# A gated decoder of sixteen blocks on one core: first three layers and last layer reordered, weight splits behind the second mixing, first attention tile's exponential in two halves

## The chip, the cores and the metric

One NeuronCore of one Trainium2 chip runs the whole program in one launch. The metric is the device time in microseconds. The kernel before took 381.14, 376.11 and 380.48 us in three runs, median 380.48.

## The reference

Two sequences of 512 tokens with 128 channels (`x`) go through four layers. Each layer is a cross attention to 77 context tokens and a feed-forward block, each behind a layer norm and a gate. In outline:

```
layer 0: bidirectional attention flow (similarity, softmax, product with tokens) | RWKV channel mix
         xk = mu_k*h + (1-mu_k)*h_prev ; r = sigmoid(xr Wr') ; out = r * (relu(xk Wk')^2 Wv')
layer 1: two-way attention with interpolation and gate                           | mixture of 8 experts, gelu, top 2
layer 2: 16-head attention with the mask                                         | mixture of 8 experts, silu, grouped top 2
layer 3: 16-head attention without a mask                                        | 8 small units relu(w1*u+b1)*w2, summed, projected
x = x + tanh(g) * block(layernorm(x))   after every block
```

All is float32 in and out.

## The kernel before, in words

The two sequences are the two halves (b = 0, 1) of every step. `x[b]` holds a half as 4 tiles of 128 tokens. A block of a half is: statistics on VectorE (DVE), the power -0.5 on GpSimd (POOL, `norm`), the normalised `h` on VectorE (`normalised`), transposes on TensorE (PE), a copy to `hT` on ScalarE (ACT, `transposed`), and then the products. Norm k and `transposed(k)` belong to block k // 2 of half k % 2.

Every engine has its program written out by hand, and each engine runs it strictly in that order. Semaphores join them. There is no scheduler; an operation whose data is ready stands behind every earlier one of its engine.

TensorE's order mixes the halves and holds filler matmuls (`keep_busy(bank, n)`, `heat` in the rows, L1443), whose result nobody reads, in places where it would otherwise wait.

The expert stages. Expert weights are loaded by SyncE (SP) into `up_raw`, `down_raw`. ScalarE rounds them (`up_hi`, `down_hi`), GpSimd makes the rests (`split_up` L460, `split_down` L467), and each product is three matmuls (L1436 to L1438). In step g VectorE makes the rest of an activation (`rlo`, L1229). At steps 15, 16, 19 and 21 it also multiplies an expert's output by that expert's routing weights (`weigh_copied`, L1173 and L1175), and TensorE's down projection of step g waits for `rlo` of step g. The routing weights reach VectorE as rows on all partitions: SyncE stores them to DRAM (`rowd`, L337), waits until the store has landed, and loads each row to 128 partitions (`rowB`, L351).

SyncE's queue, in its order:

```
load experts 0, 1; wait q["dl"] and load experts 2, 3; wait kv["one"]
50 DMAs: pieces of the values vN of layers 2 and 3 into vals (L376), up to 77 rows x 2 x 8 each
store rowd for half 0, four rowB loads; store rowd for half 1, four rowB loads; then rows and experts in turn
```

`kv["one"]` is raised by GpSimd behind four operations that write ones into `vals` (L495). `m["split"]` is raised by VectorE in `parts`, which splits `hT` into `hhi` and `hlo` (L1127, L1128) ahead of an expert stage; its first call is `parts(6, 0)`.

In layer 0's feed-forward block `mixed(b)` makes the two mixed inputs by L1012 (difference), L1013 (key) and L1015 (receptance). `l1["x"]` counts the mixed inputs, two per half.

In the attentions of layers 2 and 3 (`attend(n)`) eight tiles u of 128 tokens follow each other: scores (L1816), maximum and subtraction in two pairs of banks on VectorE (L1286, L1289), exponential on ScalarE (L812), ten transposes (L1829), copies (L826), product with the values (L1847).

The last block has eight units. `unit` (L887) makes them on ScalarE; `own_unit` (L1393, L1395) makes two of each half on VectorE. Four go one by one through TensorE (`direct`, L1967), four are summed on VectorE first (`summed`, L1403, L1406) and then projected (`from_sums`, L1985).

Of the kernel before, what the change touches and what calls it, by code (L numbers as in the profile page):

```python
# [82 lines left out]
def flamingo_program(nc, a, out):  # L83

    ctx = ExitStack()
    with ctx:
# [159 lines left out]
        l3 = {n: sem(f"l3_{n}") for n in ["wout", "s", "ss", "u", "ua", "ud", "up", "acc", "out"]}  # L246
# [171 lines left out]
        def _(pool):  # L418
# [155 lines left out]
        def _(act):  # L574
# [30 lines left out]
            def down_hi(i, p, chunks, nd, sems):  # L605

                if i > 0:
# [105 lines left out]
            second_T(1)  # L713
            transposed(6)
            first_exp(1)
# [74 lines left out]
            def attend(n):  # L790
# [18 lines left out]
                for u in range(NT * B):  # L809
                    T = NT * B * n + u  # L810
                    act.wait_ge(at["sub"], NG * (T + 1))
                    nc.scalar.activation(Sx[T % 2][:, 0:SPAN], Sx[T % 2][:, 0:SPAN], ACT.Exp).then_inc(at["exp"], 1)  # L812
# [76 lines left out]

            act.wait_ge(l3["ss"], 1)  # L890
# [10 lines left out]
        def _(dve):  # L901
# [64 lines left out]
            def softmax_out(b, exp_sem, P_sem, sumcol):  # L966
# [4 lines left out]
                link(V.reciprocal(small[b][:, sumcol + NT:sumcol + 2 * NT], small[b][:, sumcol:sumcol + NT]))  # L971
                V.tensor_tensor(pr, pr, small[b][:, sumcol + NT:sumcol + 2 * NT].unsqueeze(2).broadcast_to([P, NT, K]),
                                ALU.mult).then_inc(P_sem, 1)

# [34 lines left out]
            def mixed(b):  # L1009
# [4 lines left out]
                                       ALU.add).then_inc(l1["x"], 1)  # L1014
                V.scalar_tensor_tensor(W4_[b][:, :], W1_[b][:, :], col("mu_r"), hTz[b][:, 0:S], ALU.mult,  # L1015
# [53 lines left out]
            mixed(0)  # L1069
            from_outputs(1)  # L1070
            squared(0)
# [5 lines left out]
            mixed(1)  # L1077
# [310 lines left out]
            def own_unit(b, j):  # L1388

                dve.wait_ge(l3["ss"], b + 1)  # L1390
                dve.wait_ge(at["T"], 3 * (2 * NT * B - 1 + b))
                i, u = DIRECT[2 * j], Sx[b][:, j * S:(j + 1) * S]
                link(V.tensor_scalar(u, W1_[b][:, :], cols[:, C_W1 + i:C_W1 + i + 1], cols[:, C_B1 + i:C_B1 + i + 1],  # L1393
# [37 lines left out]
        def _(pe):  # L1431
# [69 lines left out]
            def output(b, tiles):  # L1501

                pe.wait_ge(l0["W"], b + 1)
                pe.wait_ge(l0["u"], b + 1)
                for t in tiles:
                    o = tile(bank[4 * b + 1], t)
                    mm(o, tile(hT[b], t), w14[b][:, :], start=True, stop=False)
                    mm(o, W2_[b][0:K, t * P:(t + 1) * P], ctxW2[:, b, :], start=False, stop=False)
# [582 lines left out]
```

## Time and profile before

| | |
|---|---|
| median of the runs | 380.48 us (376.11 to 381.14) |
| the profiled execution | 380.25 us |
| its span | 378.5 us |
| TensorE, VectorE, ScalarE, GpSimd busy | 354.4, 280.2, 213.2, 103.9 us |
| mean granted clock of TensorE | 0.985 |

The span starts at the first recorded instruction, and all times in rows count from there. TensorE's clock is given as a share of 2.4 GHz; 0.50 is 1.2 GHz. A float32 matmul is recorded in passes, so TensorE's counts are twice those of the program there. Busy times of TensorE are modelled from its records, and some records can be missing.

### The profile page before, as it was taken

How to read it: one execution, taken by the hardware profiler on the slowest of the kernel's cores; microseconds unless marked ns; L12 is line 12 of the kernel's file. 1: busy time of each engine (PE TensorE's matmuls, PEld its weight loads, DVE VectorE, ACT ScalarE, POOL GpSimd, SP SyncE). 2: the span in 40 equal slices, each digit the busy share in tenths (PEclk: the TensorE clock that was granted, in tenths of full speed). 3: DMA queues.
4: the chain of work that ended last, by engine and by line, in shares of the span. 5: the costliest groups of instructions: out<-in, count | busy, mean ns of one | idle time of the engine just before them, and what ended most of it. 6: DMA issues, size and time to landing. Idle time of an engine off the chain costs nothing. (4 is left out here: it accounts for less than half of the span.)

```text
span 378.5 us, 5695 instructions
## 1 busy us (share of the span) xinstructions
PE 354.4 (94%) x2020; PEld 266.4 (70%) x2034; DVE 280.2 (74%) x644; ACT 213.2 (56%) x389; POOL 103.9 (27%) x106
## 2 busy tenths in 40 slices
PE   6999989989999999989899999999989989999996
PEld 2667586857777888854688886667667646789765
DVE  5477978589776777786777769687767867788485
ACT  1315344567978889752466654767455514566382
POOL 6211751011344546220112101214556323000220
PEclk9999998999999999999999999999999998799999
DMA  6800120000474323000001100065350000000001
GB/s 192 291 3 0 51 66 5 4 5 4 132 217 158 90 76 82 5 0 2 0 2 43 42 2 0 0 189 163 97 167 2 0 2 0 0 3 2 0 2 55
DMA packets 18676, 20.37 MB, mean 54 GB/s; under 512 B 7119, under 2 KB 10729, under 8 KB 18649
## 3 DMA queue, kind: packets, MB, share of 16 engines
q1 hardware_dynamic: 18100, 19.52, 17.1%
q0 software_dynamic: 96, 0.32, 0.3%
q8 instruction: 16, 0.26, 0.3%
q10 hardware_dynamic: 453, 0.18, 0.2%
q14 instruction: 11, 0.09, 0.1%
HBM read 19.26 MB, written 0.59 MB: 52 GB/s over the span
## 5 line engine op out<-in xcount | busy, mean ns | idle before, releaser
L1229 DVE TENSOR_TENSOR rlo<-banks,rhi 128x512 fp32r<-128x512 f32 x64 | 44.0, 691 | 20.0 <-ACT rhi L744 19.1
L442 POOL TENSOR_TENSOR rstd<-var,neghalf 128x4 f32<-128x4 f32 x16 | 16.6, 1040 | 132.2 <-DVE var L918 132.2
L1436 PE MATMUL banks<-hhi,wuh 128*128 128x512 f32 x128 | 51.4, 402 | 0.6 <-DVE hlo L1128 0.5
L750 ACT ACTIVATE banks<-banks,b1s 128x512 f32<-128x512 f32 x64 | 42.4, 662 | 15.8 <-PE banks L1438 15.5
L1438 PE MATMUL banks<-hhi,wul 128*128 128x512 f32 x128 | 50.0, 391 | 0.0
L1437 PE MATMUL banks<-hlo,wuh 128*128 128x512 f32 x128 | 49.9, 390 | 0.0
L1436 PE MATMUL banks<-rhi,wdh 128*128 128x512 f32 x96 | 40.6, 423 | 8.2 <-DVE rlo L1229 3.4
L1443 PE MATMUL banks<-heat 128*128 128x512 bf16 x124 | 36.2, 408 | 4.1 <-POOL heat L420 2.9
L1847 PEld LDWEIGHTS banks<-vals,shared 128*128 128x128 f32 x320 | 37.7, 193 | 0.7 <-ACT shared L826 0.6
L826 ACT ACTIVATE shared<-banks 128x512 f32<-128x512 f32 (+1 forms) x48 | 23.7, 526 | 25.6 <-PE banks L1829 25.4
L1847 PE MATMUL banks<-vals,shared 128*128 128x27 f32 (+1 forms) x320 | 37.8, 271 | 0.1
L1437 PE MATMUL banks<-rlo,wdh 128*128 128x512 f32 x96 | 37.6, 391 | 0.0
L1438 PE MATMUL banks<-rhi,wdl 128*128 128x512 f32 x96 | 37.6, 391 | 0.0
L460 POOL TENSOR_TENSOR wul<-up_raw,wuh 128x512 fp32r<-128x512 f32 x16 | 21.6, 1348 | 51.9 <-ACT wuh L603 50.7
L846 ACT ACTIVATE shared<-banks 128x512 f32<-128x512 f32 x32 | 19.2, 599 | 29.4 <-PE banks L1438 29.1
L1286 DVE TENSOR_REDUCE small<-banks 128x8 f32<-128x616 f32 x32 | 25.4, 794 | 13.7 <-PE banks L1816 13.7
L1436 PEld LDWEIGHTS banks<-rhi,wdh 128*128 128x128 f32 x96 | 18.0, 187 | 22.5 <-DVE rlo L1229 7.6
L1336 DVE TENSOR_TENSOR banks<-shared,banks 128x512 f32<-128x512 f32 x32 | 22.2, 694 | 15.5 <-PE banks L1438 15.4
L1436 PEld LDWEIGHTS banks<-hhi,wuh 128*128 128x128 f32 x128 | 24.1, 188 | 7.4 <-ACT shared L846 1.3
L744 ACT ACTIVATE rhi<-banks 128x512 fp32r<-128x512 f32 x48 | 28.5, 597 | 0.0
L477 POOL TENSOR_TENSOR wb<-wb,wa 128x512 f32<-128x512 f32 x14 | 18.1, 1294 | 36.4 <-DVE wa L1189 19.5
L583 ACT ACTIVATE hTz<-banks 128x512 f32<-128x512 f32 x16 | 9.6, 600 | 32.4 <-PE banks L1449 32.3
(260 smaller groups left out, 708.8 us busy)
## 6 DMA issues: line engine op xcount, KB each, us to landing
rowB<-rowd SPq DMA_DIRECT2D x32, 256.0 KB, 4.3
up_raw<-in_w SPq DMA_DIRECT2D x8, 258.0 KB, 4.5
down_raw<-in_w SPq DMA_DIRECT2D x8, 256.0 KB, 5.1
up_raw<-in_v SPq DMA_DIRECT2D x8, 256.0 KB, 2.8
down_raw<-in_v SPq DMA_DIRECT2D x8, 128.0 KB, 3.4
mats<-in_mats SPq DMA_DIRECT2D x1, 640.0 KB, 5.5
mats<-in_mats SPq DMA_DIRECT2D x1, 576.0 KB, 4.1
x<-in_x SPq DMA_DIRECT2D x2, 256.0 KB, 3.6
```

The lines of the kernel that those rows point to most:

```text
L460: nc.gpsimd.tensor_tensor(wul[p][:, :], up_raw[p][:, 0:F1], wuh[p][:, :].bitcast(F32), ALU.subtract).then_inc(sems["ul"], 1)
L744: nc.scalar.activation(rhi[g % 4][:, :], bank[BANKS1[g % 4]][:, :], ACT.Copy).then_inc(q["hiA"], 1)
L750: nc.scalar.activation(bank[BANKS1[g % 4]][:, :], bank[BANKS1[g % 4]][:, :], ACT.Gelu, bias=b1s[p][:, c_:c_ + 1]).then_inc(q["gelu"], 1)
L826: nc.scalar.activation(PT[T % 2][:, 512 * j:512 * j + w], bank[BANKT[j]][:, 0:w], ACT.Copy).then_inc(at["PT"], 1)
L1229: V.tensor_tensor(rlo[g % 4][:, :], bank[BANKS1[g % 4]][:, :], rhi[g % 4][:, :].bitcast(F32), ALU.subtract).then_inc(q["lo"], 1)
L1286: link(V.reduce_max(mx, sc, AX))
L1336: V.tensor_tensor(bank[BANKU[g % 4]][:, :], silu[g % 2], bank[BANKU[g % 4]][:, :], ALU.mult).then_inc(r["mul"], 1)
L1436: mm(o, lh, rh, start=start, stop=False)
L1437: mm(o, lh, rl, start=False, stop=False)
L1438: return mm(o, ll, rh, start=False, stop=stop)
L1443: mm(o[:, :], heat[:, 0:P], heat[:, :], start=True, stop=True)
L1847: last = mm(bank[0][:, h0 * VW:(h0 + heads) * VW], tile(PT[T % 2], c_), vals[:, n, b, r0:r0 + heads * VW], start=(c_ == 0), stop=(c_ == CH ...
```

## The change

Nothing of the arithmetic changes but where two units of the last block are computed. The diff:

- GpSimd's first splits wait for `l1["x"]` = 4 (both halves mixed) instead of for the norm of block 2. Norms 5 and 6 come directly behind them. The ones in `vals` wait for the first `m["split"]` in addition.
- Layer 0 and 1: the similarity row, `product`, `token_sum`, `largest`, the softmax and the receptance's mixing change places; fillers are fewer. Layer 1: `transposes(5)` stands behind `context(1)`, and half 1's exponential before the copy of `hT`, its scaling behind `parts(6, 0)`.
- Attention: the exponential of tile 0 goes in two halves, each behind its own pair of banks. In `attend(1)` three fillers are added at tile 1, and two fall away at the end.
- Last block: `hidden_of(0)` ahead of `output_of(1)`, half 0's two own units on ScalarE, other orders of the units and sums.

```diff
@@ gpsimd @@
-            pool.wait_ge(ln_h, NT * 5)
+            pool.wait_ge(l1["x"], 2 * B)
             for p in range(2):
                 split_up(0, p, q)
                 split_down(0, p, C1, q)
+            norm(5)
+            norm(6)
+            pool.wait_ge(m["split"], 1)
             pool.wait_ge(ld["ident"], 16)
             pool.wait_ge(ld["const"], 16)
             for n in range(2):
...
             last.then_inc(l3["wout"], 1)
+            norm(7)
             pool.wait_ge(kv["act"], 1)
             for b in range(B):
                 key(0, b)
-            norm(5)
-            norm(6)
-            norm(7)
@@ scalar @@
-            transposed(0)
             act.wait_ge(p0_pe, 1)
             nc.scalar.activation(simrow[:, :], bank[7][0:1, 0:B * K], ACT.Identity,
                                  bias=rows[0:1, R_BSIM:R_BSIM + 1]).then_inc(p0_act, 1)
+            transposed(0)
...
+            first_exp(1)
             transposed(6)
-            first_exp(1)
...
+                    if u == 0:
+                        act.wait_ge(at["sub"], NG * T + 2)
+                        nc.scalar.activation(e[:, 0:SPAN // 2], e[:, 0:SPAN // 2], ACT.Exp).then_inc(at["exp"], 1)
+                        act.wait_ge(at["sub"], NG * (T + 1))
+                        nc.scalar.activation(e[:, SPAN // 2:SPAN], e[:, SPAN // 2:SPAN], ACT.Exp).then_inc(at["exp"], 1)
...
-            for i in (1, 0, 2, 3, 4, 7):
+            act.wait_ge(at["T"], 3 * (2 * NT * B - 1))
+            for i in (1, 0, 2):
                 unit(0, i)
+            whole_unit(0)
+            for i in (3, 4, 7):
+                unit(0, i)
+            whole_unit(1)
             transposed(15)
             hidden_in(1)
             act.wait_ge(l3["ss"], 2)
-            for i in (1, 0, 2, 3, 4, 7):
+            for i in (0, 2, 3, 4, 1, 7):
                 unit(1, i)
@@ vector @@
             token_sum(0)
+            product(0)
             largest(1)
-            product(0)
+            softmax_out(1, l0["exp"], l0["P"], 24)
             negated(1)
-            softmax_out(1, l0["exp"], l0["P"], 24)
             from_outputs(0)
             statistics(2)
+            token_sum(1)
             product(1)
-            token_sum(1)
...
-            mixed(0)
+            key_mixed(0)
             from_outputs(1)
+            receptance_mixed(0)
...
+            softmax_sums(1, l2["exp"], 32)
             parts(6, 0)
-            softmax_out(1, l2["exp"], l2["P"], 32)
+            softmax_scaled(1, l2["P"], 32)
...
             attended(1)
-            own_unit(0, 0)
+            summed(0, 0)
+            summed(0, 1)
             normalised(15)
-            own_unit(0, 1)
-            for j in range(len(SUMMED)):
-                summed(0, j)
-            own_unit(1, 0)
+            summed(0, 2)
+            summed(0, 3)
+            own_unit(0)
             last_update(0)
             summed(1, 0)
-            own_unit(1, 1)
+            own_unit(1)
@@ tensor @@
-            transposes(5)
             context(1)
             keep_busy(bank[6], 2)
+            transposes(5)
...
                     elif u == 1:
+                        if n == 1:
+                            keep_busy(bank[0], 2)
                         transpose_of(0, 1)
+                        keep_busy(bank[0], n)
                         values_of(0)
...
                 if n == 1:
                     values_of(NT * B - 1)
-                    keep_busy(bank[1], 2)
...
             output_T(1)
-            keep_busy(bank[5], 2)
+            hidden_of(0)
             output_of(1)
-            hidden_of(0)
```

The order of GpSimd's instructions from the third norm on, with what each waits for (its own order of the program). `q_uh`, `q_ul`, `q_dh` are ScalarE's and its own parts of a weight split, `kv_act` the values from ScalarE. Before:

```order
18 L442 TENSOR_TENSOR rstd<-var,neghalf 128x4 [waits ln_var] x3
19 L460 TENSOR_TENSOR wul<-up_raw,wuh 128x512 [waits q_uh,ln_h]
20 L467 TENSOR_TENSOR wdl<-down_raw,wdh 128x512 [waits q_ul,q_dh]
21 L460 TENSOR_TENSOR wul<-up_raw,wuh 128x512 [waits q_uh]
22 L467 TENSOR_TENSOR wdl<-down_raw,wdh 128x512 [waits q_ul,q_dh]
23 L495 TENSOR_SCALAR vals<-const 128x30 [waits ld_const,ld_ident]
24 L495 TENSOR_SCALAR vals<-const 128x30 x3
25 L501 TENSOR_SCALAR woutS<-mats,cols 128x128 [waits ld_ctx,ld_l3]
26 L501 TENSOR_SCALAR woutS<-mats,cols 128x128 x3
27 L453 TENSOR_TENSOR kbg<-kT,const 128x308 [waits kv_act]
28 L453 TENSOR_TENSOR kbg<-kT,const 128x308
29 L442 TENSOR_TENSOR rstd<-var,neghalf 128x4 [waits ln_var] x3
```

With the change:

```order
19 L460 TENSOR_TENSOR wul<-up_raw,wuh 128x512 [waits q_uh,l1_x]
20 L467 TENSOR_TENSOR wdl<-down_raw,wdh 128x512 [waits q_ul,q_dh]
21 L460 TENSOR_TENSOR wul<-up_raw,wuh 128x512 [waits q_uh]
22 L467 TENSOR_TENSOR wdl<-down_raw,wdh 128x512 [waits q_ul,q_dh]
23 L442 TENSOR_TENSOR rstd<-var,neghalf 128x4 [waits ln_var] x2
24 L498 TENSOR_SCALAR vals<-const 128x30 [waits ld_const,ld_ident,m_split]
25 L498 TENSOR_SCALAR vals<-const 128x30 x3
26 L504 TENSOR_SCALAR woutS<-mats,cols 128x128 [waits ld_ctx,ld_l3]
27 L504 TENSOR_SCALAR woutS<-mats,cols 128x128 x3
28 L442 TENSOR_TENSOR rstd<-var,neghalf 128x4 [waits ln_var]
```

The ones in `vals` (L495, now L498) stand behind two norms and one more wait. SyncE's queue has the same instructions in the same order as before.

TensorE at the start of the last block: L1449 are transposes of `h`, L1855 those of the attention's result, L1861 its output projection, L1961 the block's input product, L1967 the direct units. Before:

```order
909 L1443 MATMUL banks<-heat 128x512 x2
910 L1449 MATMUL banks<-const,h 128x128 x4
911 L1855 MATMUL banks<-const,wa 128x128 x4
912 L1443 MATMUL banks<-heat 128x512 x2
913 L1861 MATMUL banks<-mats,wb 128x128 x4
914 L1961 MATMUL banks<-hTz,mats 128x512
915 L1443 MATMUL banks<-heat 128x512 x5
916 L1967 MATMUL banks<-woutS,wd 128x128 x4
```

With the change:

```order
911 L1484 MATMUL banks<-const,h 128x128 x4
912 L1897 MATMUL banks<-const,wa 128x128 x4
913 L2005 MATMUL banks<-hTz,mats 128x512
914 L1903 MATMUL banks<-mats,wb 128x128 x4
915 L2011 MATMUL banks<-woutS,wd 128x128 x4
916 L1478 MATMUL banks<-heat 128x512 x5
```

The input product of half 0 has moved ahead of the output projection of half 1, and the two pairs of fillers are gone.

## Rows read from the trace of the kernel before

**Rows 1.** The page: busy time by engine.

```profile
PE 354.4 (94%) x2020; PEld 266.4 (70%) x2034; DVE 280.2 (74%) x644; ACT 213.2 (56%) x389; POOL 103.9 (27%) x106
```

**Rows 2.** Busy time and granted clock by stretches; columns in the first row.

```profile
core 0: us, PE busy (x) PEld busy (x) DVE busy (x) ACT busy (x) POOL busy (x), PEclk, DMA share, GB/s
56.00:60.00 4.00, 3.53 (x12) 2.74 (x14) 3.86 (x12) 1.17 (x3) 0.00 (x0) 0.57 0.07 4
102.00:114.00 12.00, 11.80 (x52) 9.20 (x51) 10.07 (x16) 9.62 (x17) 5.15 (x4) 1.00 0.65 195
320.00:326.00 6.00, 6.00 (x26) 3.67 (x30) 3.56 (x6) 1.80 (x3) 0.92 (x1) 0.50 0.00 0
```

**Rows 3.** Timeline of SyncE's queue: start, us, instruction, count.

```profile
48.74 42.13 SPq L376 DMA_DIRECT2D vals<-vN  x50
94.14 0.32 SPq L337 DMA_DIRECT2D rowd<-cT  x1
95.64 1.76 SPq L351 DMA_DIRECT2D rowB<-rowd  x4
```

**Rows 4.** Timeline of GpSimd; in brackets idle time before and its releaser.

```profile
41.36 1.68 POOL L460 TENSOR_TENSOR wul<-up_raw,wuh 128x512 fp32r<-128x512 f32 x1 [1.23 <-DVE h L925]
...
47.77 0.82 POOL L495 TENSOR_SCALAR vals<-const 128x30 f32<-128x30 f32 x4
...
60.58 1.01 POOL L442 TENSOR_TENSOR rstd<-var,neghalf 128x4 f32<-128x4 f32 x1 [4.86 <-DVE var L918]
```

**Rows 5.** Timeline of VectorE around the first row products.

```profile
65.30 0.69 DVE L1128 TENSOR_TENSOR hlo<-hTz,hhi 128x512 fp32r<-128x512 f32 x1
...
100.92 0.68 DVE L1173 TENSOR_TENSOR wb<-wa,rowB 128x512 f32<-128x512 f32 x1
101.79 0.69 DVE L1229 TENSOR_TENSOR rlo<-banks,rhi 128x512 fp32r<-128x512 f32 x1 [0.19 <-ACT rhi L744]
...
106.21 0.68 DVE L1173 TENSOR_TENSOR wb<-wc,rowB 128x512 f32<-128x512 f32 x1
```

**Rows 6.** By source line: issues of `vals` pieces; landing of `rowB` loads, 94 to 104.

```profile
L376 SPq DMA_DIRECT2D vals<-vN x50: 635/812/1062, 48.7 to 90.0; - x50
...
DMA to landing us min/median/max: 3.1/3.7/4.3
```

**Rows 7.** Timeline of TensorE: the down projection of step 16.

```profile
102.63 0.47 PE L1436 MATMUL banks<-rhi,wdh 128*128 128x512 f32 x1
```

**Rows 8.** Timeline of TensorE: transposes of layer 1.

```profile
56.25 1.15 PE L1449 MATMUL banks<-const,h 128*128 128x128 f32 x4 [1.08 <-DVE h L925]
```

**Rows 9.** Timeline of VectorE: the mixing of half 0, then of half 1.

```profile
31.29 0.75 DVE L1013 SCALAR_TENSOR_TENSOR wb<-wa,cols,hTz 128x512 f32<-128x512 f32 x1
...
41.92 1.67 DVE L1013 SCALAR_TENSOR_TENSOR wb<-wa,cols,hTz 128x512 f32<-128x512 f32 x1
43.51 1.75 DVE L1015 SCALAR_TENSOR_TENSOR wd<-wa,cols,hTz 128x512 f32<-128x512 f32 x1
```

**Rows 10.** Timelines of ScalarE and TensorE: first tiles of both attentions.

```profile
178.60 1.23 ACT L812 ACTIVATE Sx<-Sx 128x1232 f32<-128x1232 f32 x1 [5.40 <-DVE Sx L1289]
...
180.18 1.04 PE L1829 MATMUL banks<-const,Sx 128*128 128x128 f32 x8
...
310.48 3.63 PE L1443 MATMUL banks<-heat 128*128 128x512 bf16 x16
...
316.69 0.44 PE L1829 MATMUL banks<-const,Sx 128*128 128x128 f32 x2 [0.31 <-ACT shared L826]
```

**Rows 11.** Timelines of TensorE and ScalarE in the last block.

```profile
357.08 1.16 PE L1861 MATMUL banks<-mats,wb 128*128 128x128 f32 x8 [0.28 <-ACT wb L805]
358.07 1.02 PE L1961 MATMUL banks<-hTz,mats 128*128 128x512 f32 x2
...
366.89 1.06 PE L1967 MATMUL banks<-woutS,wc 128*128 128x128 f32 x8
...
360.58 1.51 ACT L887 ACTIVATE up_raw<-wa,cols 128x512 f32<-128x512 f32 x2
```

More of the change, by code:

```diff
@@ L245, in flamingo_program @@
               ["q", "qT", "S", "sub", "exp", "T", "PT", "O", "norm", "OT", "OTs", "out"]}
-        l3 = {n: sem(f"l3_{n}") for n in ["wout", "s", "ss", "u", "ua", "ud", "up", "acc", "out"]}
+        l3 = {n: sem(f"l3_{n}") for n in ["wout", "s", "ss", "u", "ua", "uo", "ud", "up", "acc", "out"]}
         nb_ready = sem("nb_ready")
@@ L810, in attend @@
                     T = NT * B * n + u
-                    act.wait_ge(at["sub"], NG * (T + 1))
-                    nc.scalar.activation(Sx[T % 2][:, 0:SPAN], Sx[T % 2][:, 0:SPAN], ACT.Exp).then_inc(at["exp"], 1)
+                    e = Sx[T % 2]
+                    if u == 0:
[3 more added lines that the diff above has]
+                        nc.scalar.activation(e[:, SPAN // 2:SPAN], e[:, SPAN // 2:SPAN], ACT.Exp).then_inc(at["exp"], 1)
+                    else:
+                        act.wait_ge(at["sub"], NG * (T + 1))
+                        nc.scalar.activation(e[:, 0:SPAN], e[:, 0:SPAN], ACT.Exp).then_inc(at["exp"], 1)
                     if u == 1:
@@ L1516, in _ @@
             pe.wait_ge(ready_const, 1)
+            pe.wait_ge(ld["ctx"], 48)
+            mm(bank[7][0:1, 0:B * K], col("w2"), ctxT[:, :], start=True, stop=True).then_inc(p0_pe, 1)
             transposes(0)
-            pe.wait_ge(ld["ctx"], 48)
             pe.wait_ge(ld["l0"], 16)
-            mm(bank[7][0:1, 0:B * K], col("w2"), ctxT[:, :], start=True, stop=True).then_inc(p0_pe, 1)
             for b in range(B):
@@ L1828, in transpose_of @@
                     for c_ in ((0, 1, 2, 3, 4, 5, 6, 7), (8, 9))[part_]:
+                        if u == 0 and c_ == 4:
+                            pe.wait_ge(at["exp"], exponentials(0))
                         last = nc.tensor.transpose(tile(bank[BANKT[c_ // 4]], c_ % 4), tile(Sx[T % 2], c_), ident)
@@ L1961, in hidden_of, with direct, from_whole, from_dve @@
                 mm(bank[3][:, :], mat("WinD"), hT[b], start=True, stop=True).then_inc(l3["s"], 1)
-            def direct(b, j, u, ready, count):
+            def direct(b, j, u, ready, count, first=False):
                 pe.wait_ge(ready, count)
                 for t in range(NT):
-                    mm(tile(bank[1 + b], t), tile(u, t), woutS[:, j, :], start=(j == 1 and t == 0), stop=False)
+                    last = mm(tile(bank[1 + b], t), tile(u, t), woutS[:, j, :], start=(first and t == 0),
+                              stop=(b == 1 and j == 3 and t == NT - 1))
+                if b == 1 and j == 3:
+                    last.then_inc(l3["out"], 1)
             def from_act(b):
-                direct(b, 1, W4_[b], l3["ua"], b + 1)
-            def from_dve(b, j):
-                direct(b, 2 * j, Sx[b][:, j * S:(j + 1) * S], l3["ud"], 2 * b + j + 1)
-            def from_pool(b):
+                direct(b, 1, W4_[b], l3["ua"], b + 1, b == 0)
+            def from_whole(j):
+                direct(0, 2 * j, Sx[0][:, j * S:(j + 1) * S], l3["uo"], j + 1)
+            def from_dve(j):
+                direct(1, 2 * j, Sx[1][:, j * S:(j + 1) * S], l3["ud"], j + 1, j == 0)
+            def from_last(b):
                 direct(b, 3, W3_[b], l3["up"], b + 1)
@@ L1984, in from_sums @@
                 for t in range(NT):
-                    last = mm(tile(bank[1 + b], t), tile(W2_[b], t), mat("WoutD"), start=False, stop=(t == NT - 1))
-                last.then_inc(l3["out"], 1)
+                    last = mm(tile(bank[1 + b], t), tile(W2_[b], t), mat("WoutD"), start=False,
+                              stop=(b == 0 and t == NT - 1))
+                if b == 0:
+                    last.then_inc(l3["out"], 1)
             output_T(1)
-            keep_busy(bank[5], 2)
+            hidden_of(0)
             output_of(1)
-            hidden_of(0)
             pe.wait_ge(l3["wout"], 1)
             pe.wait_ge(at["sub"], NG * NT * B * 2)
+            from_act(0)
             keep_busy(bank[5], 5)
-            from_act(0)
-            keep_busy(bank[5], 3)
-            from_dve(0, 0)
-            keep_busy(bank[5], 2)
+            from_whole(0)
+            keep_busy(bank[5], 5)
             transposes(15)
-            keep_busy(bank[5], 3)
+            from_last(0)
             pe.wait_ge(l3["ss"], 1)
             hidden_of(1)
-            from_dve(0, 1)
-            from_pool(0)
+            from_whole(1)
             from_sums(0)
             keep_busy(bank[5], 2)
+            from_dve(0)
+            keep_busy(bank[5], 2)
+            from_dve(1)
+            keep_busy(bank[5], 2)
             from_act(1)
-            from_dve(1, 0)
-            from_pool(1)
-            from_dve(1, 1)
-            keep_busy(bank[5], 3)
             from_sums(1)
+            from_last(1)
 def shape_constants():
```

51 lines of the change are left out of this document (33 added, 18 removed).

## The prediction

> **What bounds the kernel now.** I read the page first, then the granted clock by stretches, then each engine's timeline where the diff touches it, and last SyncE's queue, since one moved step releases DMAs. TensorE is busy for 354.4 of 378.5 us [rows 1], and 11.80 of 12 us in the first expert stage [rows 2]. So a microsecond that TensorE loses there is not found again, and one that it gains must come out of the few holes of the first layers and the last. The chain of waits reaches back only into the last layer and says nothing of the middle.
>
> The queue of SyncE is the row to look at. Its fifty DMAs into `vals` are issued back to back from 48.74 us and take 42.13 us to issue, until 90.87. Behind them in the same queue stands the store of the routing weights (`rowd`), which goes out at 94.14, when ScalarE has the weights. At 95.64 its data has landed and the row loads (`rowB`) start [rows 3]. The queue is thus free only 3.3 us before it is wanted.
>
> **Weight splits behind the second mixing.** The fifty DMAs wait for `kv["one"]`, which GpSimd raises behind four small operations on `vals`. These end at 47.77 + 0.82 = 48.59 [rows 4], and the first DMA follows 0.15 us later. In the change GpSimd runs them only behind norm 5, norm 6 and a wait for `m["split"]`, the first split of an activation by VectorE. Norm 6 alone starts at 60.58 [rows 4]. The split's last operation ends at 65.30 + 0.69 = 65.99 [rows 5]. The queue then goes, on the old clock of the trace:
> - 65.99, GpSimd reacts in about 0.06, four operations 0.82, first DMA 0.15 later: 67.02.
> - Fifty issues at 635 to 1062 ns, median 812 [rows 6], in sum 42.13: 109.15. They are issue time of one queue, in a stretch in which the DMA engines do almost nothing, so I see nothing that would shorten them.
> - The `rowd` store, wanted at 94.14, goes out at 109.15. Its landing takes 95.64 - 94.14 = 1.50, so the first row load goes out at 110.65.
> - A row load lands 3.1 to 4.3 us after its issue, median 3.7 [rows 6]: 114.35.
>
> VectorE multiplies by the first row at 100.92, in its program order behind residual 15 and ahead of residual 16 (start 101.79) [rows 5]. It waits there 114.35 - 100.92 = 13.4 us, and everything behind it waits as well. TensorE needs residual 16 for the down projection that starts at 102.63 [rows 7]. It may run one more hidden product ahead, as before, and then stops. VectorE had 0.2 us of waiting of its own between the row product and residual 16, so TensorE loses **13.2 us**. ScalarE's work is in hand by then, GpSimd stands behind VectorE. The second half's rows are not late a second time: their store goes out with the first four loads (1.76), lands after 1.5, and with 3.7 more is there some 3.3 us behind the first row. VectorE wants it 5.3 us behind (106.21) [rows 5].
>
> The bounds of this term: the landing alone gives 12.6 to 13.8. If the issues all went at the shortest seen, 0.635 us, the series would take 31.8 and the wait would be 3.1. If at the longest, 53.1, it would be 24. I take the sum as it was measured, for it is the same list of DMAs.
>
> On the price of an issue a rule speaks against this. The Trainium skill, DMA: Bandwidth & Descriptors, section on the anatomy of one DMA (the GpSimd path), puts the sequencer's dispatch at about 50 ns and says that many descriptors can be emitted before their number is felt. By that fifty DMAs would be an estimated 2.5 us and the queue would be free long before it is wanted. The trace disagrees, with 812 ns each on SyncE.
>
> **The clock after the wait.** In the trace a hole of 1.08 us in front of the transposes at 56.25 [rows 8] lies just ahead of a stretch of four microseconds with a mean granted clock of 0.57 [rows 2]. That is 3.4 us at the lower level (1.2 GHz, 0.50). Another such stretch is 6 us long, 320 to 326 [rows 2]. TensorE will stand for some 12 us now, so it comes back at the lower level. At half speed 3.4 to 6 us cost 1.7 to 3 us where it is the bound. I take **2.0**, near the shorter one, because dense matmuls follow.
>
> **First layers.** Two things can be gained. The splits run beside the second mixing: its two fused operations took 1.67 and 1.75 us, where the same kind took 0.75 [rows 9]. That is 1.9 us too much, with GpSimd's splits from 41.36 on [rows 4]. And the hole of 1.08 us at 56.25 gets the context matmuls moved into it. The reordered outputs of layer 0 let VectorE's product and the next sums start some tenths earlier. Against this, fewer filler matmuls stand in the waits, GpSimd's splits now meet the small operations behind the mixing, and TensorE is nearly full already. Upper bound 3.0 (1.9 and 1.1), lower bound a loss of 1, the price of a few cold microseconds. I take **-1.5**, half of the upper bound. It survives the wait above, since the queue's start is counted from the split, which comes earlier by as much.
>
> For the mixing the Trainium skill, SBUF — State Buffer, section on the two separate sides, says that VectorE with two SBUF inputs and GpSimd hold a shared port pair for a whole instruction, and the other blocks. The trace agrees (1.67 against 0.75). By that rule the splits would block the later two-input operations in turn, and of the 1.9 us a part would come back as other waits.
>
> **Exponential in halves.** The whole one ends at 178.60 + 1.23 = 179.83, and TensorE reaches the transposes at 180.18 behind other work [rows 10]. The halves cost ScalarE an instruction and free nothing: **0**. In the second attention three fillers are added (0.227 us each, 3.63 for 16) next to a wait of 0.31 [rows 10], and two are taken out at its end. They may keep the clock up through 320 to 326. Those 6 us at 0.50 are worth up to 3.0, less 0.4 of fillers outside the wait. Bounds -2.6 and +0.4; I take the middle, **-1.3**, as no row shows whether so small a filling is enough.
>
> **Last layer.** The input product of half 0 moves ahead of the output projection of half 1: it started 358.07 - 357.08 = 0.99 us behind it [rows 11], and ScalarE's chain of units starts that much earlier. Two units of half 0 move from VectorE to ScalarE (1.51 us for two there) [rows 11], which eats a part, but VectorE's sums set the end and lose two units. The last product, however, now stands behind the sums, with some 0.9 to 1.1 us on TensorE [rows 11]. Bounds -1.8 and +0.8, I take **-0.9**.
>
> **Sum.** The profiled execution took 380.25 us. 380.25 + 13.2 + 2.0 - 1.5 + 0 - 1.3 - 0.9 = **391.8**. The median of the runs shown is 380.48, practically the same, but they spread from 376.11 to 381.14. I call 2% (388.1 and above, or 372.9 and below) what a measurement can tell from no change.
>
> **Rivals.**
> - *The queue keeps up* (8%). If SyncE issues the list at the shortest pace seen, the wait is 3.1 instead of 13.4, TensorE loses 2.9 and hardly cools (0.5), and the gains show: 380.25 + 2.9 + 0.5 - 3.7 = 380. For it speaks that pieces of one and two rows were issued in near 0.64. Against it: most pieces have 49 to 77 rows, and nothing about them changes. It decides if the series ends before about 96, that is in under 29 us; only then the time drops to 377.
> - *The splits only* (3%): that the fifty DMAs do not hang on the moved wait. The order of the program says they do.
> - *A long cold stretch, or a second late row* (9%). The clock stays low for 6 us and more and the rows of the second half are late by 2: 396.
> - *Cold first layers* (5%). With fewer fillers TensorE drops to the lower level there and the -1.5 becomes +2: 395.
> - *Forecast* (75%): 388.5 to 394.5.
>
> The range is 387 to 396. Under 387 lie the first two rivals and a little of the forecast's lower edge. Slower by over 2%: 0.85 (forecast nearly whole, third and fourth rival). Within 2%: 0.13. Faster: 0.02, if the queue keeps up and all gains are at their bounds.
>
> **What would show it.** In the changed profile: the first `vals` DMA at 64 to 67 us instead of 48.7, the last at 106 to 109, the `rowd` store right behind it. VectorE's first product with `rowB` has some 13 us of idle time in front, released by a DMA, and TensorE's clock is at 0.50 for some microseconds after it. The mixing of half 1 takes 0.75 per operation. The forecast is wrong if that idle time is under 8 us, or if the series of fifty takes clearly less than 42 us.

## The result, and the profile after

| | before | change |
|---|---|---|
| median of the executions | 380.21 us (4) | 394.62 us (4: 390.44 to 405.25) |
| the profiled execution | 380.25 us | 391.60 us |
| its span | 378.5 us | 389.8 us |

The ratio of change to before is 1.033, with a 95% interval of 1.025 to 1.041: slower. The forecast was 391.8: 0.2 above the profiled execution and 2.8 below the median. Here and in the experiments the ratios leave out executions over 1.5% above the fastest of their kernel; medians and ranges hold all of them. Of the four executions of the change two took 397.63 and 405.25 us, with a mean granted clock of 0.961 and 0.940 where the profiled one has 0.977. No trace of these two is kept, so it stays open in which stage they lost the time.

SyncE's queue in the change, to be held against [rows 3]:

```profile
66.54 42.12 SPq L376 DMA_DIRECT2D vals<-vN  x50
108.70 0.48 SPq L337 DMA_DIRECT2D rowd<-cT  x1
110.36 1.76 SPq L351 DMA_DIRECT2D rowB<-rowd  x4
112.17 0.33 SPq L337 DMA_DIRECT2D rowd<-cT  x1
116.18 8.08 SPq L351 DMA_DIRECT2D rowB<-rowd  x8
```

The series of fifty starts 17.8 us later and takes the same 42.1 us. The store that went out at 94.14 in the kernel before stands behind it and goes out at 108.70. What released the series is in GpSimd's timeline, to be held against [rows 4]: the ones wait for the first split (`hlo`).

```profile
65.54 0.97 POOL L498 TENSOR_SCALAR vals<-const 128x30 f32<-128x30 f32 x4 [4.55 <-DVE hlo L1162]
```

VectorE, against [rows 5]. The row arrives, and the first product with it has 12.62 us of idle time in front:

```profile
100.50 0.69 DVE L1264 TENSOR_TENSOR rlo<-banks,rhi 128x512 fp32r<-128x512 f32 x1 [1.56 <-ACT rhi L745]
113.81 0.69 DVE L1207 TENSOR_TENSOR wb<-wa,rowB 128x512 f32<-128x512 f32 x1 [12.62 <-DMA rowB<-rowd]
114.42 0.68 DVE L1264 TENSOR_TENSOR rlo<-banks,rhi 128x512 fp32r<-128x512 f32 x1
...
120.00 0.68 DVE L1207 TENSOR_TENSOR wb<-wc,rowB 128x512 f32<-128x512 f32 x1
```

TensorE, against [rows 7]. It starts its last hidden product at 102.54, stands 12.31 us for the rest of the activation (`rlo`), which VectorE makes behind that row product, and comes back with matmuls 0.43 us apart where they were 0.23 apart:

```profile
102.54 0.40 PE L1473 MATMUL banks<-hhi,wul 128*128 128x512 f32 x1
115.25 0.77 PE L1471 MATMUL banks<-rhi,wdh 128*128 128x512 f32 x1 [12.31 <-DVE rlo L1264]
115.81 0.63 PE L1472 MATMUL banks<-rlo,wdh 128*128 128x512 f32 x1
...
118.80 0.56 PE L1473 MATMUL banks<-rhi,wdl 128*128 128x512 f32 x1
119.19 0.39 PE L1471 MATMUL banks<-hhi,wuh 128*128 128x512 f32 x1
```

In the table by stretches (columns as in [rows 2]) the clock falls inside the wait and recovers at about 119. A stretch at 0.50 is called cold in what follows, one at 1.00 warm.

```profile
102.00:108.00 6.00, 0.94 (x5) 0.41 (x3) 0.00 (x0) 2.73 (x5) 1.26 (x1) 0.79 0.07 4
108.00:116.00 8.00, 0.75 (x2) 0.69 (x3) 2.19 (x4) 0.00 (x0) 0.22 (x1) 0.50 0.52 137
116.00:120.00 4.00, 4.00 (x13) 3.12 (x12) 2.20 (x5) 1.17 (x2) 1.05 (x1) 0.61 0.57 184
```

**Where the 11.35 us of the two profiled executions lie.** VectorE's residual updates (`x`, sixteen of them, each adding a block to the tokens) cut the span into stages. Before:

```profile
76.01 0.75 DVE L930 SCALAR_TENSOR_TENSOR x<-wd,tg,x 128x512 f32<-128x512 f32 x1
162.97 0.74 DVE L930 SCALAR_TENSOR_TENSOR x<-banks,tg,x 128x512 f32<-128x512 f32 x1
...
301.20 0.74 DVE L930 SCALAR_TENSOR_TENSOR x<-banks,tg,x 128x512 f32<-128x512 f32 x1
...
348.42 0.75 DVE L930 SCALAR_TENSOR_TENSOR x<-banks,tg,x 128x512 f32<-128x512 f32 x1 [0.55 <-PE banks L1861]
```

And in the change:

```profile
75.48 0.75 DVE L950 SCALAR_TENSOR_TENSOR x<-wd,tg,x 128x512 f32<-128x512 f32 x1
176.72 0.74 DVE L950 SCALAR_TENSOR_TENSOR x<-banks,tg,x 128x512 f32<-128x512 f32 x1
...
315.57 0.74 DVE L950 SCALAR_TENSOR_TENSOR x<-banks,tg,x 128x512 f32<-128x512 f32 x1
...
360.67 0.75 DVE L950 SCALAR_TENSOR_TENSOR x<-banks,tg,x 128x512 f32<-128x512 f32 x1 [0.55 <-PE banks L1903]
```

Differences of these starts, and the span's end, give the stages. The same was read from the profiles of the experiments (in us); each row is one execution.

| kernel | first layers | first experts | between | second attention | last block |
|---|---|---|---|---|---|
| before | 76.01 | 86.96 | 138.23 | 47.22 | 30.08 |
| the change | 75.48 | 101.24 | 138.85 | 45.10 | 29.13 |
| ones in front again (e1) | 78.46 | 87.31 | 140.57 | 51.22 | 29.14 |
| ones late alone (e2) | 75.01 | 102.03 | 139.07 | 45.22 | 30.07 |
| list divided (e3) | 73.53 | 87.61 | 140.15 | 54.42 | 29.19 |
| smaller dose (e4) | 73.54 | 97.62 | 139.90 | 45.09 | 29.15 |
| fillers in attention (e5) | 74.54 | 86.97 | 139.82 | 45.22 | 30.05 |
| first layers alone (e13) | 82.04 | 86.41 | 138.24 | 45.63 | 30.08 |
| later splits alone (e8) | 76.15 | 87.46 | 139.79 | 45.22 | 29.98 |
| last block alone (e6) | 75.86 | 86.38 | 138.70 | 46.05 | 29.51 |
| exponential in halves (e7) | 76.32 | 86.83 | 139.90 | 45.49 | 30.06 |
| divided, old fillers in attention (e11) | 78.47 | 87.13 | 138.31 | 45.09 | 29.50 |
| divided, hole filled (e10) | 81.64 | 87.35 | 138.27 | 45.09 | 29.15 |
| mended: as e10, four fillers back in layer 0 (e12) | 74.61 | 87.81 | 138.27 | 45.09 | 29.12 |

The stage of the first experts holds the loss (+14.28). The others give back 2.98 in sum (-0.53, +0.62, -2.12, -0.95). The column "between" takes either 138.2 to 138.9 or 139.1 to 140.6 us; the longer ones have a few microseconds at the lower clock there (in 220 to 226 us of e5, for example), whichever edits the kernel has.

### The profile page after: what moved, and what is told of

Same layout as the page of the kernel before. It is cut to its first block and busy times, and to the rows that moved or that the text cites. A ratio compares the mean times of both kernels' runs of the same rounds, so it can differ in the third digit from the quotient of the medians.

```text
span 389.8 us, 5666 instructions
## 1 busy us (share of the span) xinstructions
PE 350.4 (90%) x2008; PEld 265.1 (68%) x2022; DVE 278.1 (71%) x640; ACT 214.4 (55%) x393; POOL 102.7 (26%) x106
## 5 line engine op out<-in xcount | busy, mean ns | idle before, releaser
L1478 PE MATMUL banks<-heat 128*128 128x512 bf16 x112 | 31.8, 398 | 3.8 <-POOL heat L420 2.9
L460 POOL TENSOR_TENSOR wul<-up_raw,wuh 128x512 fp32r<-128x512 f32 x16 | 20.7, 1294 | 53.4 <-ACT wuh L604 50.1
L1473 PEld LDWEIGHTS banks<-hhi,wul 128*128 128x128 f32 x128 | 24.2, 189 | 5.3
```

The lines of the kernel that those rows point to most:

```text
L460: nc.gpsimd.tensor_tensor(wul[p][:, :], up_raw[p][:, 0:F1], wuh[p][:, :].bitcast(F32), ALU.subtract).then_inc(sems["ul"], 1)
L1473: return mm(o, ll, rh, start=False, stop=stop)
L1478: mm(o[:, :], heat[:, 0:P], heat[:, :], start=True, stop=True)
```

## Experiments

Stages are named as in the table; "before" is always the kernel before on the same chip, in the same comparison. The first four ask whether the wait is the whole loss, and on what its size hangs.

**e1: the ones back in front.** GpSimd raises `kv["one"]` right behind the weight splits; the rest of the change stays.

```diff
+            (the four ones on vals, kv["one"])
             norm(5)
             norm(6)
-            pool.wait_ge(m["split"], 1)
```

> The changed kernel, but the ones in vals (and with them kv["one"]) stand directly behind the four weight splits, as before, without the wait for m["split"]. Queue theory: the cost is SyncE's list of fifty DMAs, which starts behind kv["one"]. GpSimd's last split ends at about 48.6, so the list runs from about 49.5 to 91.7, the rowd store goes out when the weights are ready (about 94), VectorE does not wait for a row. The 14.3 us are gone: 376.5 to 378 us. Rival, GpSimd: what costs is what the later place of the splits and norms does to VectorE and TensorE; then the time stays above 388. Rival, first layers: the new order of layers 0 and 1 costs; above 388 too.

Median 381.33 us (377.55 to 388.49, 11 executions), before 378.57, ratio 1.004 [1.000, 1.008]. The series starts at 52.24, the store goes out at 97.32, and the row product has no wait. The stage of the first experts is back at 87.31. So of the change's 3.3% some 2.9 (11 us) hang on this place of the ones. The time itself is 3 us above what I expected: the gain that the rest was to bring does not show, and by the ratio the rest costs 0.4%. The profile has some 10 us at the lower clock in the first layers (16 to 28) and some 14 in the second attention (330 to 346).

**e2: the ones late, and nothing else.** The kernel before, with norms 5 and 6 and the wait for the split put ahead of the ones.

```diff
+            norm(5)
+            norm(6)
+            pool.wait_ge(m["split"], 1)
             (the four ones on vals, kv["one"])
...
-            norm(5)
-            norm(6)
             norm(7)
```

> The kernel before with only this moved: norms 5 and 6, then the wait for the first m["split"], then the ones in vals; the splits stay where they were. Queue theory: the list starts at 66 + 0.8 + 0.2 = 67.0 and ends at 109.1, first row at about 114, VectorE waits 13 us, TensorE comes back at the lower clock for 3 to 4 us: 380.2 + 13.2 + 1.7 = 395, range 393 to 397. Rivals (the splits' place, or the new order of the first layers): 380 to 382, since neither is in this kernel.

392.82 us (392.56 to 393.18), ratio 1.035 [1.033, 1.038]. This is the slowdown of the whole change, from the ones alone being raised later; it came out 2.2 us below what I expected, just under the range. The row product of this kernel:

```profile
113.60 0.69 DVE L1174 TENSOR_TENSOR wb<-wa,rowB 128x512 f32<-128x512 f32 x1 [12.85 <-DMA rowB<-rowd]
```

**e4: a smaller dose.** The change without the wait for the split: the ones follow norm 6.

```diff
             norm(5)
             norm(6)
-            pool.wait_ge(m["split"], 1)
```

> The changed kernel without the wait for m["split"]: the ones come behind norm 6 (end at about 61.0), 4.5 us earlier. Queue theory, in doses: the list runs from 62.1 to 104.2, the wait for the first row shrinks from 12.6 to about 8.2, the cold stretch behind it stays: 391.0 - 4.5 = 386.5, range 385.5 to 388. If the wait cost by a threshold or by the split alone, it would be 377 or 391.

389.12 us (387.07 to 391.71), ratio 1.026 [1.020, 1.031]. The wait came out as the sum over the queue has it:

```profile
107.49 0.69 DVE L1206 TENSOR_TENSOR wb<-wa,rowB 128x512 f32<-128x512 f32 x1 [8.21 <-DMA rowB<-rowd]
```

The series starts at 60.10, which is 6.4 us earlier than in the change, and the wait is 4.4 shorter. The two differ because the row is also wanted earlier: 99.28 here (107.49 - 8.21), 101.19 in the change (113.81 - 12.62). The median came out 2.6 us above what I expected, the profiled execution (387.07) 0.6. Behind the wait TensorE needs 6.1 us at the lower clock (14 matmuls from 108.93 to 115.02) and not 3.9 as in the change, which costs about 1 us of it. Why the other executions are longer is open.

**e3: the list divided.** The change, but SyncE issues only the 25 pieces of layer 2 early; those of layer 3, wanted after 300 us, go out behind the row loads of the first expert stage.

```diff
-            for n in range(2):
+            def scatter_values(n):
                 (wait kv["act"], 25 DMAs)
+            scatter_values(0)
...
                     next_row(0, 4 * i + j)
+            scatter_values(1)
```

> The changed kernel, GpSimd's program untouched (ones late), but SyncE issues only the 25 pieces of layer 2's values at the old place; the 25 of layer 3 come behind the row loads of the first expert stage. Queue theory: 25 issues are 21 us, from 66.5 to 87.6, ahead of the store at about 94; nobody waits: 376.5 to 378 us, as with the ones early. Rival, GpSimd: its order is the slow one still, so 390 to 392.

380.72 us (374.97 to 391.68, 10 executions), ratio 0.995 [0.991, 1.000]. The ratio rests on the five executions up to 380.21; the median of all ten is 2.2 us above the kernel before. With the late start kept (64.59), the wait is gone, because the list is half as long:

```profile
64.59 21.17 SPq L376 DMA_DIRECT2D vals<-vN  x25
92.35 0.31 SPq L337 DMA_DIRECT2D rowd<-cT  x1
```

The stage of the first experts takes 87.61 us, so the late release harms through the length of what it releases ahead of the store. But the executions now lie up to 17 us apart, and the profiled one (386.64) has some 20 us at the lower clock in the second attention (326 to 347). The next runs look for what scatters.

**e13: the first layers alone.** The kernel before with the change's edits on ScalarE, VectorE and TensorE in the first three layers; fillers from 3 + 2 + 2 + 4 to 1 + 0 + 1 + 1 in the attention of layer 0, and one fewer behind it.

```diff
-            keep_busy(bank[6], 3)
+            keep_busy(bank[6], 1)
             token_products(0)
...
-            token_max_everywhere(1)
-            keep_busy(bank[6], 2)
             output(0, range(NT))
```

> The kernel before with the reordering of the first three layers alone (ScalarE, VectorE, TensorE with its fewer fillers); GpSimd's splits, the list of 50, the second attention and the last layer stay. Theory A: there is a gain of some 1.5 us up to the update of half 1 in the second block, and in a part of the executions it is lost again and more, because with eight fillers fewer the clock falls between 18 and 35 us; the times spread from 376.5 to 383 and the median is 0 to 2 us above the kernel before. Theory B (the fall comes from elsewhere): a plain gain of 1.5, 376.5 to 377.5, with no more spread than the kernel before.

382.78 us (378.53 to 386.87, 11 executions) against 378.13, ratio 1.009 [1.006, 1.013]. The median is 4.7 us above, where I expected up to 2. No execution had a mean granted clock above 0.991; of the 34 of the kernel before in the same comparison 21 had. Its stretches:

```profile
16.00:20.00 4.00, 3.92 (x21) 2.90 (x22) 2.04 (x8) 1.35 (x4) 0.00 (x0) 0.78 0.34 125
20.00:28.00 8.00, 8.00 (x36) 7.27 (x34) 3.07 (x9) 0.66 (x3) 0.00 (x0) 0.50 0.01 3
28.00:36.00 8.00, 7.76 (x33) 6.60 (x35) 4.14 (x19) 0.77 (x2) 1.02 (x1) 0.54 0.00 0
```

Some 17 us are cold, and the first layers take 82.04 us instead of 76.01. TensorE was busy for 3.92 of the 4 us in which the clock fell, so no large hole in front explains it; in the kernel before it was busy for the same 3.92 there, and the clock stayed at 1.00. The change's own profile has a shorter one (clock 0.54 in 20 to 22, after a hole of 0.38 at 19.79), and the profiles of e1, e10 and e11 have it as well; those of e3 and e4 do not, and there the first layers take 73.5. All profiles with the old fillers (before, e2, e5, e6, e7, e8) stay at 1.00 from 16 to 36 us.

**e6: the last block alone.**

```diff
-            for i in (1, 0, 2, 3, 4, 7):
+            for i in (1, 0, 2):
                 unit(0, i)
+            whole_unit(0)
...
             from_act(1)
-            from_dve(1, 0)
-            from_pool(1)
-            from_dve(1, 1)
-            keep_busy(bank[5], 3)
             from_sums(1)
+            from_last(1)
```

> The kernel before with the last layer's reordering alone. My prediction's term is a gain of 0.9, which the profile of the change bears out from the last update of the block before to the end: 377.5 to 378, with the spread of the kernel before. Rival: TensorE's last product, now one behind the sums, makes it longer in most executions, and the gain is 0 (378.5).

377.49 us (375.98 to 383.15), ratio 0.997 [0.995, 0.999], a gain of 1.2 us with an interval from 0.3 to 2.0. In the table the stage gains 0.57, in the change itself 0.95. The rest goes with another edit: e6 and e11 keep the old fillers of the second attention, two of them at its end, and take 29.51 and 29.50 us in this stage; the change, e1, e3, e4, e10 and e12 have the new ones and take 29.12 to 29.19. With the old order of the last block (e5) the new fillers bring nothing here, 30.05.

**e7: the halves alone.**

```diff
+                    if u == 0:
+                        act.wait_ge(at["sub"], NG * T + 2)
+                        nc.scalar.activation(e[:, 0:SPAN // 2], ...)
```

> The kernel before with the first tile's exponential in two halves alone, in both attentions. My prediction's term is 0: the same time within 0.3 us. Rival: the second attention's first transposes start earlier, TensorE's small wait there goes and 0.3 us are gained; or the halves cost ScalarE 0.2 us more and the copies behind them come later, 0.3 us lost.

377.14 us (376.11 to 380.37), ratio 0.998 [0.996, 1.000]. That is 0.8 us less, with an interval that nearly touches zero, and no stage of its profile shows a gain that is not the clock's. I leave it at zero to a few tenths; where a gain would come from is not shown.

**e8: the later splits alone.**

```diff
-            pool.wait_ge(ln_h, NT * 5)
+            pool.wait_ge(l1["x"], 2 * B)
```

> The kernel before, with only GpSimd's first weight splits made to wait for the second mixing; the ones still stand right behind the splits. Theory A (contention on the port moves and is not removed): the two mixing operations fall from 1.67 and 1.75 to 0.75 us, but VectorE's small operations behind them grow by about 1 us in sum, the list of 50 starts at some 50 instead of 48.7 and still ends ahead of the store of the routing weights, and the time is that of the kernel before within 0.7 us. Theory B (my prediction's upper bound): the gain of 1.9 us on VectorE reaches the end, 1 to 2 us below the kernel before.

379.18 us (377.40 to 383.86), before 378.50, ratio 0.999 [0.996, 1.003]: nothing gained. VectorE's timeline says why, against [rows 9]:

```profile
41.79 0.75 DVE L1013 SCALAR_TENSOR_TENSOR wb<-wa,cols,hTz 128x512 f32<-128x512 f32 x1
42.46 0.75 DVE L1015 SCALAR_TENSOR_TENSOR wd<-wa,cols,hTz 128x512 f32<-128x512 f32 x1
44.15 0.69 DVE L1034 TENSOR_REDUCE small<-banks 77x1 f32<-77x512 f32 x1 [0.94 <-PE banks L1615]
44.87 1.12 DVE L1035 TENSOR_TENSOR small<-small,kshift 77x1 f32<-77x1 f32 x1
46.02 1.19 DVE L1036 TENSOR_TENSOR small<-kshift,small 77x1 f32<-77x1 f32 x1
47.13 0.46 DVE L961 TENSOR_REDUCE small<-banks 128x4 f32<-128x308 f32 x1
```

and GpSimd's, with the splits:

```profile
44.70 1.27 POOL L467 TENSOR_TENSOR wdl<-down_raw,wdh 128x512 fp32r<-128x512 f32 x1
45.93 1.26 POOL L460 TENSOR_TENSOR wul<-up_raw,wuh 128x512 fp32r<-128x512 f32 x1
```

In the kernel before the last three of VectorE's were

```profile
45.89 0.50 DVE L1035 TENSOR_TENSOR small<-small,kshift 77x1 f32<-77x1 f32 x1
46.43 0.15 DVE L1036 TENSOR_TENSOR small<-kshift,small 77x1 f32<-77x1 f32 x1
46.51 0.47 DVE L961 TENSOR_REDUCE small<-banks 128x4 f32<-128x308 f32 x1
```

The mixing sheds 1.92 us. The two operations on one column of 77 numbers grow from 0.50 and 0.15 to 1.12 and 1.19: each ends when one of GpSimd's splits does (44.70 + 1.27, 45.93 + 1.26). 1.66 of the 1.92 come back there, and 0.94 more go into a wait for TensorE. VectorE reaches the next step (L961) at 47.13 and not at 46.51: alone, the later splits cost 0.6 us there and gain nothing. That is theory A, to which the wait for TensorE has to be added.

**e5: the second attention's fillers alone**, and **e11: the divided list with the old fillers there.**

```diff
                     elif u == 1:
+                        if n == 1:
+                            keep_busy(bank[0], 2)
                         transpose_of(0, 1)
+                        keep_busy(bank[0], n)
```

> The kernel before, with only the second attention's fillers changed (three more fillers at its tile 1, two fewer at its end). Theory A: the fillers keep the clock up where the kernel before had six cold microseconds (320 to 326), but TensorE then arrives early at the scores of tile 3 and stands there some 1.1 us for VectorE, and the clock falls behind that hole instead. How long it stays low differs from execution to execution: the times scatter from 376 to 388, against 377 to 380.5 before, and the median lies within 1.5 of the kernel before. Theory B, my prediction's: the fillers simply gain 1.3 to 2.6, 377 to 378.5 with no more scatter than before, and the scatter of the changed kernel comes from its last layer or its first layers.

> The change with SyncE's list divided (25 pieces early, 25 behind the row loads of the first expert stage, as in the run with the divided queue) and with the old fillers in the second attention. Theory A (the fillers make the scatter): the times lie within 3 us of each other, at 377 to 378.5, with six cold microseconds in the middle of the second attention and none behind. Theory B (something else makes it): the times scatter from 375 to 388 as they did with the divided queue alone.

e5: 378.87 us (376.00 to 394.31), ratio 0.998 [0.994, 1.001]. e11: 380.42 us (377.93 to 383.83), ratio 1.005 [1.002, 1.008]. The fillers bring no gain that shows. Of e5's 12 executions five lie above 382, and of the 35 of before beside it six. This leans to theory A, but twelve executions are too few to show it. And e5's own profile has the clock at 1.00 and the hole of 1.09 us, and so has e8's with the old fillers: the hole exists whenever that stretch runs warm, the fillers did not make it. e5 takes 45.22 us in the second attention, e2 and e8 with the old fillers take the same. e11 missed as well, 2 us above what I expected; in its profile the second attention is warm with the old fillers (45.09, as in the change), and the first layers are cold for some 10 us (first x update at 26.86, against 22.34 in e3).

**e10: the hole filled**, and **e12: the hole and the first layer filled.** Both on top of the divided list.

```diff
                     pe.wait_ge(hT_ready, base + b + 1)
+                    keep_busy(SIDE, 4 * n * b)
                     mm(SIDE[:, :], mat(wq), hT[b] ...)
```

e12 also has the lines

```diff
-            keep_busy(bank[6], 1)
+            keep_busy(bank[6], 3)
             token_products(0)
...
+            keep_busy(bank[6], 2)
             output(0, range(NT))
```

> The change with SyncE's list divided, and four fillers (some 0.9 us) between the second attention's tile 1 and the queries of the second half, in the hole of 1.09 us in front of the scores of tile 3. Theory A (the fall of the clock hangs on that hole): the hole shrinks to 0.2 us, no cold stretch follows in the second attention, and the times are 375 to 376.5 with under 3 us between them. Theory B (the clock falls for another reason, the hole is only near it): a stretch at 0.50 of 7 us and more in the second attention stays in the profile, and the times scatter up to 388.

> The change with SyncE's list divided, four fillers in the hole ahead of the scores of tile 3 of the second attention, and four of the removed fillers back in the first layer (two ahead of the first token products, two ahead of the first output). Theory A (the cold stretches hang on missing fillers): neither place falls cold, and the times are 375 to 377, under the kernel before, with 2 us between them. Theory B (the fall is not a matter of these fillers): the times stay as with the filled hole alone, 378 to 385.

e10: 381.56 us (378.16 to 385.71), ratio 1.004 [1.000, 1.009]. The hole shrank from 1.09 to 0.31 and the second attention stayed warm, but the first layers were cold for some 17 us and no time came in as expected (the lowest is 378.16). e12: 376.72 us (375.37 to 378.07, 12 executions) against 378.13, ratio 0.996 [0.994, 0.998]: the lowest median of the study, and the least scatter but for e2 with its four executions. Theory A has it, but for 1 us at the upper end. Its stretch where e13 was cold:

```profile
20.00:28.00 8.00, 7.67 (x57) 6.51 (x57) 6.03 (x26) 0.98 (x3) 1.02 (x1) 1.00 0.01 3
28.00:36.00 8.00, 7.52 (x54) 5.84 (x53) 6.49 (x19) 4.80 (x12) 1.01 (x1) 1.00 0.00 0
```

e10 and e12 differ in the four fillers of layer 0 alone, and their medians by 4.8 us (each against its before: 1.004 and 0.996). They ran on two chips, in two comparisons. But the mean granted clock divides them as well: 0.973 to 0.989 in the twelve of e10, 0.991 to 1.000 in the twelve of e12; and e13, without these fillers and on the chip of e12, has 0.969 to 0.991.

## Why the prediction was right, step by step

What carried it is the queue, the wait and the clock behind it (+15.2 forecast): e2, which has these alone, is 14.3 us above its before. The gains (-3.7 forecast) did not come: e1, which has all of the rest, is 2.8 us above its before by the medians and 0.4% by the ratio. The change is 14.4 us above the kernel before by the medians and 11.35 in the two profiled executions, against 11.5 forecast. The direction and most of the size are explained; that the sum met the profiled execution within 0.2 us is in part luck.

- **The queue and the wait (+13.2).** Right, by its own steps. Ones behind the split: 65.54 (65.99 + 0.06 forecast). Series 42.12 (42.13). Store 108.70 (109.15). Row wait on VectorE 12.62 (13.4), on TensorE 12.31 (13.2). The 0.8 too much: the store stood 0.45 earlier, the row was there 3.45 behind its issue (113.81 - 110.36) and not 3.7, and it was wanted at 101.19 and not 100.92; the store's landing took 0.16 more. The starts that were run (48.74 and 52.24: no wait; 60.10: 8.21; 66.23: 12.85; 66.54: 12.62) and the halved list are what makes this shown and not only argued. The rule of the Trainium skill that the forecast set beside it (DMA: Bandwidth & Descriptors, the anatomy of one DMA) had no part in the sum; it is stated there for the GpSimd path, and the issue on SyncE stayed at a median of 812 ns.
- **The second half's row** was not late a second time: 120.00, with no wait on a DMA, as forecast. The margin was thinner than it had it. Its store went out at 112.17 and its loads at 116.18, 4.0 us later and not 1.5; with the median of 3.7 to landing that is an estimated 119.9.
- **The clock after the wait (+2.0).** Right in the change. TensorE is cold from 115.25 to about 119: nine matmuls take 3.94 us (to 119.19) instead of nine times 0.23, which is 1.9 more. Wait and clock make 14.2 of the stage's 14.28. But the size is not fixed, and does not grow with the wait: 5.2 us cold behind 12.58 in e2, 6.1 behind 7.93 in e4. And the hole of 1.08 us from which the forecast read it stands in e2 and e5 too (1.08 and 1.07), with no cold stretch behind it.
- **First layers (-1.5).** There is a gain where the clock holds: 73.53 and 73.54 in e3 and e4, against 75.01 and 74.54 in e2 and e5, which have the old order and no cold stretch there either. That is 1.0 to 1.5 us, but up to 1 us of it lies ahead of the first x update, where profiles of one and the same order differ by as much (22.80 to 23.79). In the change's profile it came out at -0.53, since a cold stretch took a part. Alone (e13) the edits cost 0.9%. The step that was wrong is the chance of the rival "cold first layers", 5%: five of seven profiles with the fewer fillers have it, from 3 to 17 us long. It did not carry the profiled execution out of the range, nor the median; 397.63 and 405.25 of the four lie above it, for a reason that no trace shows.
- **The splits' 1.9 us.** The forecast took it as gain by half. The step that failed is that the other half would reach the end: in e8 the operations give back 1.66 of 1.92 and a wait for TensorE takes 0.94, a loss of some 0.6. Here the other side of the argument was right. The Trainium skill, SBUF — State Buffer, section on the two separate sides, has it that where VectorE's operation has two SBUF inputs, whichever of the two engines starts first gets the shared port pair for its whole instruction. The trace agrees, with two one-column operations at 1.12 and 1.19 instead of 0.50 and 0.15, each ending with GpSimd's split.
- **The hole ahead of the transposes (-1.1 at most).** It went, and in its place stands a smaller one, two steps on:

```profile
55.55 1.10 PE L1484 MATMUL banks<-const,h 128*128 128x128 f32 x4
57.33 1.08 PE L1651 MATMUL banks<-hTz,Mk 128*77 128x512 f32 x2 [0.69 <-ACT hTz L584]
```

- **Exponential in halves (0).** Nearly: -0.8 with an interval from -1.6 to -0.1 alone (e7), while no stage of the profile gains.
- **Second attention (-1.3).** The two profiles differ by 2.12, but not by the fillers. The six cold microseconds of [rows 2] come and go: with the old fillers e6, e7 and e13 have shorter ones there (45.49 to 46.05 in this stage), while e2 and e8 ran warm and took 45.22, as e5 did with the new fillers. e11, the change with the old fillers, takes 45.09, and the change 45.10. So the fillers are worth nothing that shows in a warm stage, and the mistake was to take a stretch of one profile for a property of the kernel. That they keep the clock up is not shown either: with the new ones e1 and e3 had a cold stretch of 14 and 20 us in this stage. Whether the hole in front of tile 3 causes it is open: it shrank in e10 and e12, whose two profiles are warm there, but so are most others. In the working, the middle of the bounds -2.6 and +0.4 is -1.1 and not -1.3; the sum would be 392.0.
- **Last block (-0.9).** Right in size: -0.95 in the profile, -1.2 [-2.0, -0.3] alone. Some 0.4 of the 0.95 comes only together with the new fillers of the second attention (29.51 without them in e6), which the forecast booked in that stage alone.

The sum was right for the profiled execution (391.8 against 391.60) partly since small errors cancel: wait and clock 15.2 against 14.3, first layers and second attention -2.8 against -2.65, and 0.6 more in the stages between, for which there was no step. And the -2.12 of the second attention is almost all a cold stretch that the profiled execution of the kernel before happened to have.

## What to carry to other kernels

An engine that issues DMAs is a queue with a price for each issue, here a median of 812 ns. Before a release is moved, add up the issue time of all that it lets go and look for what stands behind it in the same queue. If the late release must stay, shorten the list ahead of the urgent transfer. And read the clock of a stage in several executions before its cold microseconds are booked as something to win, or fillers are taken out.

## What was not expected of the hardware

- With nine fillers fewer (0.2 us each) the clock fell for up to 17 us, in a stretch where TensorE was busy for 3.92 of 4 us. It did so in five of seven profiles and in none of the six with the old fillers. With four of them put back it stayed at 1.00 in the profile, and twelve executions ranged from 375.37 to 378.07 where they had ranged from 378.16 to 385.71 (on another chip).
- How long it stays low is not a constant: 3.9, 5.2 and 6.1 us after waits of 12.3, 12.6 and 7.9 us, and 3, 10 and 17 us in the first layers of kernels with the same TensorE order there. What ends it isn't shown by any run here.
- An operation of VectorE on 77 numbers took 1.19 us instead of 0.15, beside one of GpSimd on 128x512, and ended with it.
